# A decoder's masked cross attention: weights and context split into float32r halves and weighed one slot later, the heads' low halves first in VectorE's slot, and block scales with factors read from SBUF

## The reference

```python
def cross(h, ctx, mask, Wq, Wk, Wv, Wo):              # 16 heads of 128, 8 key/value heads
    q = (h @ Wq).reshape(B, T, 16, 128).transpose(0, 2, 1, 3)
    k = (ctx @ Wk).reshape(B, Tc, 8, 128).transpose(0, 2, 1, 3); k = repeat(k, 2, axis=1)
    v = (ctx @ Wv).reshape(B, Tc, 8, 128).transpose(0, 2, 1, 3); v = repeat(v, 2, axis=1)
    scores = where(mask, einsum('bhtd,bhsd->bhts', q, k) / sqrt(128), -inf)
    out = einsum('bhts,bhsd->bhtd', softmax(scores), v)
    return out.transpose(0, 2, 1, 3).reshape(B, T, 2048) @ Wo

def mx_dequant(t):                                     # blocks of 32
    scales = maximum(max(abs(blocks), axis=-1) / 448, 1e-30)
    return (blocks / scales).astype(float8_e4m3fn).astype(float32) * scales
x = x + cross(layernorm(x), ctx, mask, ...)
h = silu(q(ln) @ q(Wg).T) * (q(ln) @ q(Wu).T);  x = x + q(h) @ q(Wd).T     # q = mx_dequant
```

## Time and profile before

| what | us |
|---|---|
| device time, median of 3 runs | 1590.79 (1587.90 to 1593.18) |
| the profiled execution, its own time | 1586.01 |
| its span in the profile | 1583.2 |
| PE busy in the span | 1482.6 (94%) |
| DVE / ACT / POOL busy | 1037.3 / 964.4 / 723.1 |
| scores of slot 0 to the last output projection of the masked cross attention | 1045.6 to 1395.3 |
| MXFP8 MLP | 1396.9 to 1583.2 |

### The profile page before, as it was taken

The page is one execution under the profiler, slowest core; times in us unless marked ns, Lnnn a source line. Parts: engine busy times, 40 slices in busy tenths (PEclk is TensorE's granted clock), DMA queues, the critical chain, the costliest instruction groups (busy, mean ns, idle before and its releaser), DMA issues. The chain is left out here.

```text
span 1583.2 us, 30060 instructions
## 1 busy us (share of the span) xinstructions
PE 1482.6 (94%) x10192; PEld 1202.2 (76%) x10192; DVE 1037.3 (66%) x2404; ACT 964.4 (61%) x2595; POOL 723.1 (46%) x877
## 2 busy tenths in 40 slices
PE   6999889999999999899997898799999999989998
PEld 2666568888888888688874555489999999967886
DVE  4667667777777777554545777655566665588886
ACT  2766657777777777533326777567777777642221
POOL 3666635555554555233333343213444444457775
PEclk9999999999999999999998999999999999999999
DMA  6000020000000000000002000020000000000000
GB/s 243 2 1 2 2 94 5 3 3 5 3 5 3 5 3 3 23 1 1 1 19 116 1 2 2 1 104 8 8 8 8 2 7 5 1 1 14 14 14 14
DMA packets 15608, 29.80 MB, mean 19 GB/s; under 512 B 1505, under 2 KB 12002, under 8 KB 14690
## 3 DMA queue, kind: packets, MB, share of 16 engines
q1 hardware_dynamic: 15458, 27.89, 4.8%
HBM read 25.79 MB, written 2.10 MB: 18 GB/s over the span
## 5 line engine op out<-in xcount | busy, mean ns | idle before, releaser
L1412 POOL TENSOR_TENSOR weights_even<-weights_even,cross_reciprocal 128x512 f32<-128x512 f32 x64 | 66.7, 1042 | 202.6 <-DVE cross_reciprocal L1644 202.6
L921 POOL TENSOR_TENSOR weights_odd_early<-weights_odd_early,cross_reciprocal 128x512 f32<-128x512 f32 x64 | 66.6, 1041 | 198.0 <-DVE cross_reciprocal L1059 198.0
L1494 ACT ACTIVATE weights_even<-bank,cross_shift 128x128 f32<-128x128 f32 x256 | 90.7, 366 | 79.8 <-DVE cross_shift L1636 79.8
L1122 PEld LDWEIGHTS bank<-ident,weights_odd_early 128*128 128x128 f32 x768 | 94.2, 141 | 45.4 <-issue 32.9
L1122 PE MATMUL bank<-ident,weights_odd_early 128*128 128x128 f32 x768 | 116.0, 274 | 3.0 <-DVE weights_odd_early L1042 2.4
L962 ACT ACTIVATE weights_odd_early<-bank,cross_shift,cross_q_rms 128x128 f32<-128x128 f32 x256 | 113.5, 455 | 2.2 <-DVE cross_shift L1036 2.2
L2436 DVE TENSOR_REDUCE grouped_maxima<-bank 128x4 bf16<-128x512 f32 x128 | 82.4, 685 | 34.8 <-PE bank L2518 27.2
L1921 POOL TENSOR_TENSOR mlp_low_inner<-mlp_inner,mlp_high_inner 128x512 fp32r<-128x512 f32 x36 | 48.7, 1354 | 117.1 <-ACT mlp_high_inner L1964 117.1
L1634 DVE TENSOR_REDUCE cross_maxima<-bank 128x4 f32<-128x512 f32 x64 | 44.2, 690 | 84.4 <-PE bank L1777 84.4
L401 POOL TENSOR_TENSOR causal_masked_maxima<-causal_maxima,causal_constants 128x512 bf16<-128x512 bf16 x64 | 67.0, 1068 | 56.0 <-DVE causal_maxima L546 56.0
L955 ACT ACTIVATE weights_odd_early<-bank 128x512 f32<-128x512 f32 x64 | 38.3, 599 | 86.8 <-PE bank L1122 86.8
(11 more groups left out here) (358 smaller groups left out, 5248.6 us busy)
## 6 DMA issues: line engine op xcount, KB each, us to landing
weights_odd_early<-in_weights SPq DMA_DIRECT2D x2, 3072.0 KB, 15.2
weights_even<-in_weights SPq DMA_DIRECT2D x2, 2560.0 KB, 11.7
weights_even<-in_weights SPq DMA_DIRECT2D x2, 1732.0 KB, 8.9
weights_odd_late<-in_weights SPq DMA_DIRECT2D x2, 1536.0 KB, 10.5
x<-in_x SPq DMA_DIRECT2D x4, 512.0 KB, 8.1
out<-mx_result SPq DMA_DIRECT2D x16, 128.0 KB, 1.7
weights_even<-in_weights SPq DMA_DIRECT2D x2, 512.0 KB, 5.6
cross_context<-in_context SPq DMA_DIRECT2D x16, 64.0 KB, 1.8
```

The lines of the kernel that those rows point to most:

```text
L921: pool.tensor_tensor(probs[x], probs[x], reciprocal[x][:, :].unsqueeze(2).to_broadcast([P, PER, P]), ALU.mult).then_inc(probs_divided, 1)
L1122: last = pe.transpose(bank[:, j * P:(j + 1) * P], source, core.ident[:, :])
L1412: pool.tensor_tensor(probs[x], probs[x], reciprocal[x][:, :].unsqueeze(2).to_broadcast([P, JOBS, P]), ALU.mult).then_inc(probs_divided, 1)
L1494: last = act.activation(probs[x][:, j, :], bank_scores[x][:, j * P:(j + 1) * P], ACT.Exp, scale=SCALE, bias=shift[x][:, j:j + 1], accum_ou ...
```

## The change

In the masked cross attention:

- The weighing becomes float32r. The transposed weights (probsT) are split: ACT copies the high half where it copied the whole, and DVE makes the low half in a new instruction (`make_low_probsT`, 128x512), placed behind the reciprocals. The context is split once a pair (high half on ACT in g = 4, low half on POOL in g = 6). Two float32 matmuls become six float32r ones.
- PE weighs group i-2 in slot i, where it weighed i-1, and adds the output of i-3, where it added that of i-2.
- The high and low halves of the heads are those of i-3 (it was i-2), and in DVE's slot the low half now stands ahead of the row maxima.
- `bank_probsT` is free again for `turn_probs` only when the low half has been made; the load of the next context waits for its low half.
- Some scratch tensors move into a region of the weights that is no longer read.

In `dve_scale` and `inverse_h` the two numbers are read from a 128x2 tensor in SBUF, written once by POOL in the set-up. This reaches the MLP too.

```diff
+def dve_block_scale(dve, core, scratch):
+    return dve.tensor_scalar(scratch.scale[:, :], scratch.largest[:, :], core.scale_bounds[:, 0:1],
+                             core.scale_bounds[:, 1:2], ALU.mult, ALU.max)
...
-    step(dve.tensor_scalar(scratch.scale[:, :], scratch.largest[:, :], 1.0 / FP8_MAX, least, ALU.mult, ALU.max))
+    step(dve_block_scale(dve, core, scratch))
...
+            def low_context(p, s):                                   # POOL
+                pool.wait_ge(context_high, p + 1)
+                pool.tensor_tensor(context_halves[s][1][:, :, :], context[s][:, :, :],
+                                   context_halves[s][0][:, :, :].bitcast(F32), ALU.subtract).then_inc(context_low, 1)
...
-                act.activation(probsT[x], four(bank_probsT), ACT.Copy).then_inc(probsT_ready, 1)
+                act.activation(probsT[x][0][:, :, :], four(bank_probsT), ACT.Copy).then_inc(probsT_high, 1)
...
-                    if there(i - 2):
-                        copy_high_heads(i - 2, g % 2)
+                    if there(i - 3):
+                        copy_high_heads(i - 3, (g - 1) % 2)
+                    if g == 4 and pair_there(t + 1) and i >= 0:
+                        copy_high_context(t + 1, 1 - s)
...
+            def make_low_probsT(i, x):                               # DVE
+                dve.wait_ge(probsT_high, i + 1)
+                dve.tensor_tensor(probsT[x][1][:, :, :], four(bank_probsT), probsT[x][0][:, :, :].bitcast(F32), ALU.subtract)\
+                   .then_inc(probsT_low, 1)
...
+                    if there(i - 3):
+                        make_low_heads(i - 3, (g - 1) % 2)
                     if there(i):
                         row_maxima(i, g % 2)
...
-                    if there(i - 2):
-                        make_low_heads(i - 2, g % 2)
...
                         reciprocals(i, g % 2)
+                    if there(i - 1):
+                        make_low_probsT(i - 1, (g - 1) % 2)
...
                 pe.wait_ge(probs_divided, i + 1)
-                pe.wait_ge(probsT_ready, nonneg(i))
+                pe.wait_ge(probsT_low, nonneg(i))
...
-                    pe.wait_ge(context_loaded[s], loads(p, s))
-                pe.wait_ge(probsT_ready, i + 1)
+                    pe.wait_ge(context_low, p + 1)
+                pe.wait_ge(probsT_low, i + 1)
                 pe.wait_ge(heads_low, nonneg(i))
                 for k in range(BOTH):
-                    last = pe.matmul(bank_out[:, k * PER * P:(k + 1) * PER * P], context[s][:, k, :],
-                                     probsT[x][:, k * PER:(k + 1) * PER, :].rearrange("p h q -> p (h q)"),
-                                     start=True, stop=True)
+                    for m, (a, b) in enumerate(PARTS):
+                        last = pe.matmul(bank_out[:, k * PER * P:(k + 1) * PER * P], context_halves[s][a][:, k, :],
+                                         probsT[x][b][:, k * PER:(k + 1) * PER, :].rearrange("p h q -> p (h q)"),
+                                         start=(m == 0), stop=(m == len(PARTS) - 1))
...
-                    if there(i - 2):
-                        add_output(i - 2, g2 % 2, p2, s2, g2)
-                    if there(i - 1):
-                        weigh_context(i - 1, g0 % 2, p0, s0, g0)
+                    if there(i - 3):
+                        add_output(i - 3, g3 % 2, p3, s3, g3)
+                    if there(i - 2):
+                        weigh_context(i - 2, g2 % 2, p2, s2, g2)
```

54 lines of the change are left out of this document (34 added, 20 removed).

## The result

The changed kernel takes 1620.86 us (median of four, 1619.95 to 1622.47) against 1591.99 us for the kernel before (four, 1587.90 to 1596.33): ratio 1.0198, 95% interval 1.017 to 1.0226. It is slower by 28.9 us. The forecast was 1612, the range 1598 to 1626: the time lies inside the range, 2 us above the 1600 to 1619 to which the forecast gave its 0.72. The profiled execution of after took 1620.68 with a span of 1618.9; the span of before was 1583.2, so the two traces differ by 35.7 us, 7 more than the medians: the profiled execution of before lies 6.0 under its median.

A forecast was written before the change was run, and what follows sets the result against it. PE bounded the kernel before; a new latency loop through ACT and DVE would set the attention's pace. Loop +21.9, start -0.5, drain +1, MLP -1 give +21.4 on the median 1590.8: 1612 us, range 1598 to 1626.

The forecast's parts named there:

- The loop that the change closes: Masked cross attention: exponentials, probsT copy, mask, heads copy, low heads, maxima, next exponentials form a loop of 5.10 us a slot.
- The slots on top: Attention slots where DVE or POOL is later exceed 5.10 us; a pair takes 46.11, slots 2 to 63 +21.9 us.
- PE's own sum would wait at `add_output`, for low heads: Masked cross attention: PE's own 40.6 us a pair would wait 5.5 us a pair at the output projection.
- PE's part: 64 weighings in the attention: 0.72 instead of 0.87 us each, 0.15 gained a slot; PE's slot about 5.08.
- The drain: End of the attention stage: one more slot and a chain behind a slice of 2.28 us, +1 us (0 to +3).
- Rival 4: The clock falls because PE waits in the attention slots, costing tens of us in all; chance 0.01.
- The factors from SBUF: MLP's first 40 us: L761 with factors from SBUF avoids waiting for POOL, -1 us (bounds 0 and -5.5).
- The sum: Whole kernel: 21.9 - 0.5 + 1 - 1 = +21.4 us, 1612 us on the median.
- start: Start of the attention stage: slot 1 has no weighing any more, -0.5 us (bounds 0 and -0.87).
- 1 (PE stays the bound): Attention: low heads do not hold the maxima, PE's sum counts, 9.6 to 18.6 us less, 1572 to 1581; chance 0.09.
- 2 (the extras are absorbed): Attention: loop runs at 5.10, half the heavy slots' additions lie beside waits, pair 43.1, 1589 to 1594; chance 0.06.
- 3 (more is late): Attention: every shift behind a rounding waits for POOL's third step, +6.7 us, low context halves too, 1619 to 1628; chance 0.12.

The follow-up runs named there:

- e7: Changed kernel with ACT's laying of the mask put behind the next heads copy: ratio 1.0157 to the kernel before.
- e1: Changed kernel with DVE's row maxima put ahead of the low heads again: 1589.67 us, ratio 1.0006 to the kernel before.
- e3: Changed kernel with both block scale numbers as constants in the instruction again: 1614.31 us, ratio 1.0166 to the kernel before.
- v1: Changed kernel with maxima first, constants, the last weight slice later and every other slice split: 1578.04 us, ratio 0.9942 to the kernel before.
- e6: Changed kernel with the last weight slice's scaling behind the last low probabilities and low heads: 1619.2 us, ratio 1.0184 to the kernel before.

## Why the prediction was right or wrong, point by point

- **The loop that the change closes: right.** Forecast 2.94, 3.57, 4.17, 5.10; measured 2.95, 3.61, 4.22, 5.14. e7 showed that the mask is a link of it (g = 1 falls by 0.39 and g = 5 by 0.90 without it), e1 that the order closes it. But "Before, this loop was not there" makes it sound like the loss itself, and it isn't: the light slots of before were 5.04 to 5.15 long for other reasons and rise by 0.2 us a pair in all, while g = 2, 3, 4 and 7 add 3.5 of the 3.7. That the load of an engine doesn't tell was right as well: none is full (90, 63, 67 and 39%).
- **The slots on top.** By exponentials, of one pair (e3 has constants, e1 the maxima first, e7 the mask behind the heads copy):

| | g0 | g1 | g2 | g3 | g4 | g5 | g6 | g7 | pair |
|---|---|---|---|---|---|---|---|---|---|
| forecast | 5.10 | 5.10 | 6.32 | 5.56 | 6.44 | 6.05 | 5.10 | 6.44 | 46.11 |
| before | 5.15 | 5.06 | 5.55 | 5.11 | 5.55 | 6.06 | 5.04 | 5.56 | 43.08 |
| after | 5.15 | 5.14 | 6.43 | 5.66 | 6.58 | 6.06 | 5.14 | 6.58 | 46.74 |
| e3 | 5.16 | 5.14 | 6.44 | 5.65 | 6.47 | 6.07 | 5.14 | 6.46 | 46.53 |
| e1 | 5.14 | 4.89 | 5.83 | 5.06 | 5.98 | 5.16 | 4.89 | 5.98 | 42.93 |
| e7 | 5.16 | 4.75 | 6.43 | 5.66 | 6.59 | 5.17 | 5.19 | 6.59 | 45.53 |

  Each term was a little small. In g = 4 and 7 it is L761, taken at 0.17 and measured at 0.29 (e3 gives 0.11 back in each). In the others it is 0.01 to 0.11, some of it in the handing over between engines (0.66 from the heads copy to the low heads, not 0.63); no run took the rest apart. Over 61 slots this is +26.3 instead of +21.9.
- **Where PE waits: wrong.** The step "PE's own sum would wait at `add_output`, for low heads" failed. The low heads are started 1.08 after the scores (1179.58 against 1178.50), long before PE reaches the output projection. PE waits at the scores, 31.0 us, for the copied queries, since that copy follows the exponentials, which are late. The wait moved to where the loop touches PE first. This changed no number of the sum.
- **PE's part: the 0.15 a weighing was right** (six instructions from 1182.80, 0.12 apart). PE's own slot, put at 5.08 as a mean, is about 5.13: v1's pair of 41.79 has 0.74 of waits in it, and an eighth of the rest is 5.13. It would have mattered had PE stayed the bound.
- **The drain: the step that failed most.** Forecast +1, bounds 0 to +3; measured +6.4. I had seen the low half of slot 63 behind a slice, but gave that slice 2.28 us, the value of the slots in which POOL is free. In the drain POOL is rounding, and the slice takes 4.67, which costs 1.8 us of the drain (e3 against e6). The lower clock of this one execution is another 1.7 (after against e3): I had excluded it from a stretch with many short waits, and PE waits 2.38 us in one piece here. What remains, 2.9 (e6 against before), fits the slot that the later weighing adds, for which and for the slice the forecast had +1 together. Rival 4 as priced (tens of us in the stage) didn't come, but its mechanism did, there alone.
- **The factors from SBUF: wrong in sign.** Forecast -1, bounds 0 to -5.5. L143 misled me: its 404 ns for 256 elements seemed slow per element, as that of an instruction with two sources. But after's L774, with a constant, does 384 elements in 0.36 us and its L1636 does 512 in 0.42, so 0.06 for 128: 256 would take 0.30, and with the 0.12 of the two factors, which I did not know, 0.42, near L143's 0.40. So L143 fits an instruction at the faster rate with its factors on top, though no run changed L143 itself. The Trainium skill ("VectorE: DVE Perf Modes", What auto-detection actually checks) asks of the two-port mode a single source and a destination in SBUF and makes no exception for factors, and the trace agrees (1118 ns at most after, 1124 before). By it the term would have been 0, and the 0.12 an instruction that comes on top is in no row of before.
- **The sum.** 21.4 + 4.4 (loop) + 5.4 (drain) + 2.0 (MLP) + 0.1 (start) + 2.4 (scatter ahead of the stage) = 35.7, the difference of the spans. By medians it is 28.9, since the profiled execution of before lies 6.0 under its median and that of after at its own. Forecast 1612 against 1620.9: the direction, the mechanism slot by slot, and three quarters of the size (21.4 of 28.9). Of the drain's 5.4, 1.7 is the clock of the profiled execution.
- **The rivals.** 1 (PE stays the bound) and 2 (the extras are absorbed) fell with the pair of 46.74. 3 (more is late) named the time, 1619 to 1628, but not the way, g = 0 being 5.15. That was close, and the forecast's 5.10 for it partly luck: in after the shift of g = 0 begins 0.24 before POOL's third step (e + 4.93 and e + 5.17), and in g = 5, where it begins 0.21 behind the start of that step, the same wait costs 0.90.

## What to carry to other kernels

Ahead of putting an operation in front of another in one engine's queue, follow its inputs back: if they come from an engine that itself waits for the one behind it, a loop closes, whose length no busy share shows. Price a moved operation twice, once in the light slots (does a loop close?) and once in the slots where that engine's own row is the path (there it costs its full time), and look at the drain by itself, with the durations of the company that it has there. In this kernel the second price was the larger one (2.4 us a pair against 0.5, and 0.9 by way of POOL). Where low halves are needed only later (here the output projection starts 1.70 us after them, 1179.58 and 1181.28 in after), they belong behind the work that another engine is waiting for.
